# GpSimd adds half of the expert planes between the first layer and the scan, the third norm goes by logarithm and exponential, and zeros are written in the routing

## The reference, cut to what matters

```
x: 16 sequences x 256 steps x 128 features, float32 (4096 tokens)
x = x + 0.5 * ffn(layernorm(x))      # first layer
x = x + mamba(layernorm(x))          # the scan
x = x + 0.5 * ffn(layernorm(x))      # last layer, same weights as the first

ffn(x): each token goes to its 3 best of 64 experts, at most 64 tokens per expert;
        gelu(x w1 + b1) w2 + b2, times the token's gate, added up over the 3 choices
mamba(x): raw, gate = split(x W_in);  h = silu(conv(raw) + b)
          ts, B, C = split(h W_x);    dt = softplus(ts W_dt + b_dt)
          state = exp(dt * A) * state + dt * B * h     # for 256 channels x 16 states
          y = sum over states (C * state) + h * D;     out = (y * silu(gate)) W_out
```

## Time and profile before

| what | value |
|---|---|
| three runs | 808.17, 806.54, 804.46 us; median 806.54 us |
| the profiled execution | 807.02 us, of which the span of the core 805.1 us |
| mean granted TensorE clock | 0.927 of full |
| busy share of the span | PE 82%, DVE 74%, ACT 57%, POOL 62% |
| first layer, to the last scatter | 0 to 184 us |
| bridge | 184 to 235 us |
| scan | 234.76 to 595.7 us |
| last layer and output | 596 to 805 us |

### The profile page before, as it was taken

One profiled execution on the slowest core, in us unless ns is written; L12 is line 12 of the kernel. 1 busy time (PEld: TensorE's weight loads), 2 busy tenths in 40 slices (PEclk: granted clock), 3 DMA queues, 4 the chain that ended last, 5 costly groups with the idle time before them and its releaser, 6 DMA issues. The chain is left out here.

```text
span 805.1 us, 27454 instructions
## 1 busy us (share of the span) xinstructions
PE 658.1 (82%) x11512; PEld 372.2 (46%) x11512; DVE 597.1 (74%) x1004; ACT 456.3 (57%) x949; POOL 495.6 (62%) x315
## 2 busy tenths in 40 slices
PE   6538998995968889899998989878989169999955
PEld 3524554562434445454544545444546045555532
DVE  7893444453689999999999999978999944533435
ACT  2402554461787888878797987866724004445530
POOL 3104565540138999999999999989961125555520
PEclk7858999997988999999999999999999569999987
DMA  8996999627275332545445153442009708997529
GB/s 279 379 345 195 324 317 313 213 80 276 74 171 118 91 99 58 136 107 136 108 120 121 34 147 68 135 107 57 3 3 357 274 11 259 320 335 249 167 85 351
DMA packets 87971, 141.29 MB, mean 175 GB/s; under 512 B 9587, under 2 KB 34813, under 8 KB 86576
## 3 DMA queue, kind: packets, MB, share of 16 engines
q1 hardware_dynamic: 83440, 126.99, 51.5%
q0 software_dynamic: 4416, 12.65, 4.4%
HBM read 112.16 MB, written 27.71 MB: 174 GB/s over the span
## 5 line engine op out<-in xcount | busy, mean ns | idle before, releaser
L1388 POOL TENSOR_TENSOR BIG<-BIG,R 128x1024 f32<-128x1024 f32 x127 | 305.3, 2437 | 17.5 <-DVE BIG L1309 16.5
L1309 DVE TENSOR_TENSOR_SCAN BIG<-BIG,ps 128x1024 f32<-128x1024 f32 x128 | 285.5, 2269 | 16.9 <-PE ps L933 16.4
L933 PE MATMUL ps<-BIG,stack 64*32 64x128 f32 x8192 | 153.9, 279 | 32.6 <-DVE BIG L1309 21.6
L933 PEld LDWEIGHTS ps<-BIG,stack 64*32 64x32 f32 x8192 | 117.9, 107 | 106.4 <-DVE BIG L1309 71.7
L791 POOL DMA_INDIRECT y_dram<-BIG,row_idx x64 | 64.8, 1013 | 87.1 <-DVE BIG L727 45.2
L777 POOL DMA_INDIRECT R<-xn_dram,tok_idx x64 | 65.4, 1022 | 70.7 <-DVE choice L701 51.7
L727 DVE TENSOR_SCALAR BIG<-ps,row_gate 128x128 f32<-128x128 f32 x64 | 22.2, 348 | 98.7 <-remote 56.6
L1178 ACT ACTIVATE BIG<-R,An 128x510 f32<-128x510 f32 x128 | 84.2, 710 | 4.4 <-DVE BIG L1309 4.3
L1178 ACT ACTIVATE BIG<-BIG,An 128x510 f32<-128x510 f32 x128 | 83.7, 709 | 0.2
L412 ACT ACTIVATE BIG<-ps 128x128 f32<-128x128 f32 x64 | 16.9, 265 | 105.9 <-PE ps L541 76.3
L418 ACT ACTIVATE BIG<-BIG 128x512 f32<-128x512 f32 x64 | 40.0, 625 | 61.2 <-DVE BIG L718 43.3
(11 more groups left out here) (184 smaller groups left out, 908.1 us busy)
## 6 DMA issues: line engine op xcount, KB each, us to landing
BIG<-in_L_ffn_w SPq DMA_DIRECT2D x120, 512.0 KB
BIG<-dt_dram SPq DMA_DIRECT2D x32, 256.0 KB, 4.6
R<-c_dram SPq DMA_DIRECT2D x32, 256.0 KB, 7.6
R<-dt_dram SPq DMA_DIRECT2D x32, 256.0 KB, 4.8
y_dram<-zeros SPq DMA_DIRECT2D x3, 2048.0 KB, 21.7
BIG<-y_dram SPq DMA_DIRECT2D x24, 256.0 KB, 7.5
BIG<-y_dram SPq DMA_DIRECT2D x12, 512.0 KB, 8.1
y_dram<-zeros SPq DMA_DIRECT2D x6, 1024.0 KB, 8.2
```

Of the source, the lines that this page charges most:

```text
L933: last = nc.tensor.matmul(ps[CW * slot:CW * slot + CW, 2 * (st % 2) + b, :] .rearrange("p (g k s) -> p k g s", g=2, k=4)[:, k], dT[q % 2][ ...
L1309: nc.vector.tensor_tensor_scan(state[st % 3], dA[:, st % 6].rearrange("p b g t -> p (b g t)"), ps[:, u:u + 2, :].rearrange("p b n -> p (b ...
L1388: nc.gpsimd.tensor_tensor(prod[st % RP], state[st % 3].rearrange("p (b g t) -> p b g t", b=2, g=2), Cf[q % 2][:, 2 * gp:2 * gp + 2].rearra ...
```

## The change

It has three parts, all within the bridge and the places where the zeros are written.

1. **The sums of planes.** VectorE adds groups 0 and 1 by itself (three adds each). TensorE and VectorE share only groups 2 and 3, and TensorE does each in two halves (`part`). GpSimd adds groups 4 to 7 by itself (`moe_sum_pool`): each group as two halves of 256 elements, three planes each, so 24 instructions, in which one waits for the plane before of its own half. They stand at the head of GpSimd's list for the mamba layer, ahead of the first `dtu`. VectorE's statistics of group g wait for the semaphore `x_pool`. ScalarE's `decays(0)` no longer waits for the sums itself but only for the memset. On ScalarE `xt_copy(0)` now stands ahead of the second root, and both `raw_copy(0, ...)` ahead of `normalise(1)`.
2. **The third norm.** The thirteen instructions are replaced: VectorE adds epsilon (`log_root_opened`, in the old place, ahead of the first scan), ScalarE takes the logarithm and the exponential of minus half of it (`log_root_scalar`, behind `decays(3)`), and VectorE does one Newton step and the mean's term in four instructions (`log_root_closed`, behind the first scan).
3. **The zeros** of the last layer's planes are written as in the first layer: three transfers of 2 MB in SP's list of the last layer, behind the first weight loads; the six transfers in the scan are gone.

```
-SUM_GROUPS = ((1, 2, 3, 4, 5, 6, 7), (1, 3, 5))
+SUM_GROUPS = ((2, 3), (1, 3, 5))
+POOL_GROUPS = (4, 5, 6, 7)
...
+        def log_root_opened(S, i0, i1):
+            nc.vector.tensor_scalar(rs[:, 0, i0:i1], mv[:, i0:i1, 1], EPS, None, ALU.add).then_inc(S("rstd"), 1)
+        def log_root_scalar(e, S, i0, i1, n, m):
+            e.wait_ge(*S.at("rstd", n + 1))
+            nc.scalar.activation(rs[:, 2, i0:i1], rs[:, 0, i0:i1], ACT.Ln).then_inc(S("root"), 1)
+            e.wait_ge(*S.at("root", m + 1))
+            nc.scalar.activation(rs[:, 2, i0:i1], rs[:, 2, i0:i1], ACT.Exp, scale=-0.5).then_inc(S("root"), 1)
+        def log_root_closed(e, S, i0, i1, n, m):
...
+            e.wait_ge(*S.at("root", m + 2))
+            nc.vector.tensor_tensor(y, z, z, ALU.mult).then_inc(S("rstd"), 1)
...  (two scalar_tensor_tensor for y and r, one for nmr)
-            if f == 0:
-                for k in range(K):
-                    e.dma_start(y_dram[0][k * T:(k + 1) * T, :]...
+            for k in range(K):
+                e.dma_start(y_dram[f][k * T:(k + 1) * T, :]...
...
+        def moe_sum_pool(e, S, f, m):
+            g = POOL_GROUPS[m]
+            e.wait_ge(G(f"yk{PIECE[g]}"), 16 * K * (f + 1))
+            for k in range(K):
+                for half in range(2):
+                    i = 4 * g + 2 * half
+                    t = X[:, i:i + 2, :].rearrange("p i d -> p (i d)")
+                    if k:
+                        e.wait_ge(*S.at("pool_partial", 4 * m + 2 * k + half - 1))
+                    nc.gpsimd.tensor_tensor(t, t, YK[:, k, i:i + 2, :].rearrange("p i d -> p (i d)"), ALU.add)\
+                        .then_inc(S("x_pool" if k == K - 1 else "pool_partial"), 1)
...
             root_scalar(e, MST, 0, 4, 0)
             normalise(0)
+            xt_copy(0)
             root_scalar(e, MST, 4, 8, 6)
-            xt_copy(0)
-            normalise(1)
             raw_copy(0, 0)
             raw_copy(0, 1)
+            normalise(1)
...
             decays(3)
+            log_root_scalar(e, MST, 8, NI, 12, 2)
             normalise(2)
...
-            moe_sum(e, F[0], 0, 4)
-            stats(8, 20)
+            stats(8, 24)
...
-            stats(20, NI)
-            statistics(8, NI, 12)
+            stats(24, NI)
+            wait(e, "meanvar", NI)
+            log_root_opened(MST, 8, NI)
             wait(e, "pads", 4)
...
                     if run:
                         scan(STEPS * q + n)
+                    if q == 0 and n == 0:
+                        log_root_closed(e, MST, 8, NI, 12, 2)
                     if q == 0 and n < C2:
                         dt(1, n)
```

More of the change, by code:

```diff
@@ L241, in macaron @@
         w2v = w2.rearrange("(a j) (p c) d -> j p a (c d)", a=2, c=HC)
[L244 to L250, removed]
-            v, y, z, r = rs[:, 0, i0:i1], rs[:, 1, i0:i1], rs[:, 2, i0:i1], rstd[:, i0:i1]
[L253 to L261, removed]
@@ new lines, in log_root_closed @@
+        def log_root_closed(e, S, i0, i1, n, m):
+            v, y, z, r = rs[:, 0, i0:i1], rs[:, 1, i0:i1], rs[:, 2, i0:i1], rstd[:, i0:i1]
+            e.wait_ge(*S.at("root", m + 2))
+            nc.vector.tensor_tensor(y, z, z, ALU.mult).then_inc(S("rstd"), 1)
+            e.wait_ge(*S.at("rstd", n + 2))
+            nc.vector.scalar_tensor_tensor(out=y, in0=y, scalar=-0.5, in1=v, op0=ALU.mult, op1=ALU.mult)\
+                .then_inc(S("rstd"), 1)
+            e.wait_ge(*S.at("rstd", n + 3))
+            nc.vector.scalar_tensor_tensor(out=r, in0=y, scalar=1.5, in1=z, op0=ALU.add, op1=ALU.mult)\
+                .then_inc(S("rstd"), 1)
+            e.wait_ge(*S.at("rstd", n + 4))
+            nc.vector.scalar_tensor_tensor(out=nmr[:, i0:i1], in0=mv[:, i0:i1, 0], scalar=-1.0, in1=r,
+                                           op0=ALU.mult, op1=ALU.mult).then_inc(S("rstd"), 1)
@@ L985, in mamba_tensor @@
                                  start=True, stop=True)
-            for g in range(1, 3):
-                plane_sums(e, F[0], 0, g)
+            plane_sums(e, F[0], 0, 2, 0)
             e.wait_ge(M("pads"), 3)
@@ L991, in mamba_tensor @@
             transposes(0)
-            plane_sums(e, F[0], 0, 3, 0)
+            plane_sums(e, F[0], 0, 2, 1)
             raw(0, 0)
             raw(0, 1)
+            plane_sums(e, F[0], 0, 3, 0)
+            transposes(1)
             plane_sums(e, F[0], 0, 3, 1)
-            transposes(1)
-            plane_sums(e, F[0], 0, 4)
             x_proj(0)
@@ L1080, in normalise @@
                 if q < 3:
-                    wait(e, "rstd", (6, 12, 12 + NEWTON)[q])
+                    wait(e, "rstd", (6, 12, 17)[q])
                 for j in range(4):
@@ L1258, in stats @@
                 for i in range(i0, i1):
-                    if i % 4 == 0:
+                    if i % 4 == 0 and i // 4 in POOL_GROUPS:
+                        e.wait_ge(*F[0].at("x_pool", 2 * POOL_GROUPS.index(i // 4) + 2))
+                    elif i % 4 == 0:
                         e.wait_ge(*F[0].at("x", i // 4 + 1))
@@ L1264, in stats @@
                     nc.vector.bn_aggr(mv[:, i, :], st[:, i, :]).then_inc(M("meanvar"), 1)
-            def statistics(i0, i1, n):
-                wait(e, "meanvar", i1)
-                inverse_root(e, MST, i0, i1, n)
             for u in range(2):
@@ L1340, in mamba_vector @@
                 tap(1, m // 3, m % 3)
-            for g in range(5, 8):
-                moe_sum(e, F[0], 0, g)
-            e.wait_ge(*F[0].at("x", 8))
+            e.wait_ge(*F[0].at("sum", 2))
+            e.wait_ge(*F[0].at("x", 4))
+            e.wait_ge(*F[0].at("x_pool", 8))
             nc.vector.memset(dA[:, :, :, :, 0:1].rearrange("p u b g t -> p (u b g) t"), 0.0).then_inc(M("pads"), 1)
@@ L1405, in diagonal @@
                     .then_inc(M("diag_pool"), 1)
+            for m in range(len(POOL_GROUPS)):
+                moe_sum_pool(e, F[0], 0, m)
             for q in range(-2, NQ):
```

25 lines of the change are left out of this document (6 added, 19 removed).

## The result

| | before | after |
|---|---|---|
| median of 4 runs each, same chip | 807.36 us | 820.09 us |
| range | 804.46 to 811.29 | 818.57 to 826.36 |
| profiled execution: time, span | 807.02, 805.1 | 826.36, 824.6 |
| mean granted TensorE clock | 0.927 | 0.901 |

The change makes the kernel slower: the ratio is 1.0163, with an interval of 1.0102 to 1.0224. The forecast was 808.1 (803.2 to 812.2) with 0.16 for slower. Another series of runs on another chip gave 1.0120 [1.0077, 1.0162]. The profiled execution after is the longest of its four, 6.3 us over their median, so its stages show rather more of the loss than the median has.

What follows compares the result with a forecast made beforehand. Bound: full VectorE and GpSimd in the scan, a chain of hand-overs in the bridge. +1.3 and +0.3 make +1.6 us on the profiled 807.02, so 808.6; the median is 0.5 lower: 808.1, range 803.2 to 812.2.

Steps and rivals of the forecast that it cites:

- rival 2: A TensorE stall in bridge or scan goes or comes as its list shortens; 3.4 us either way, chance 0.14 for better.
- rival 3: Bridge: TensorE too idle, clock at 1.2 GHz again between 203 and 233; half of it costs 4.8 us; chance 0.16.
- The sum of the parts: Whole kernel: 1.3 us for the later second scan step plus 0.3 for GpSimd, +1.6 us.
- To the first silu: Bridge, sums up to the first silu: 1.1 us later, at 210.6 (bounds +0.5 and +1.9).
- GpSimd's adds: Bridge: 24 adds on GpSimd at 0.72 us each, 17.3 us in all, done at 218.8; cost counted 0.
- From silu to the decays: Bridge: 0.4 of the 1.1 us delay comes back, decays start at 229.8; first scan step at 233.4, 1.3 earlier.
- The third norm: Start of the scan: second step waits for ScalarE's exponential, at 240.6, 1.3 us later (bounds +0.7 and +2.1).
- GpSimd late by 0.3: Start of the scan: GpSimd's `dtu` and first product start 2.9 us later; 0.3 us added (0 to 0.8).
- The zeros: Zeros moved from the scan to the last layer: cost 0, bounds -1 and +1 us.
- the same: Whole kernel: measured time within 0.5%, 4.0 us, of before, between 802.5 and 810.6; chance 0.74.

Runs made afterwards that it cites:

- the kernel before with 205 added: The kernel before with 205 waiting TensorE instructions added, 145 in the first layer's routing and 60 in the bridge; ratio 1.0102 to the kernel before.
- with the edges back in place: The kernel after with 51 waiting TensorE instructions added in the bridge; 787.17 us, ratio 1.0019 to the kernel before on the same chip.
- With the clock kept: The kernel after with 25 matmuls on ones and one waiting instruction added in the bridge; 810.02 us, ratio 0.9996 to the kernel before.

## Why the prediction was wrong

**The step that failed is rival 2, a stall of TensorE that goes or comes.** It saw what decides: long waits with nothing named "look like instructions that came late", and with 24 matmuls and their weight loads out of the list "every later stall falls elsewhere". But it priced this as one stall, with 3.4 us either way, and gave a chance of its own only to the better side; for slower it counted on rival 3 "with some stalls". Measured, the other place cost 1.4% or about 11.6 us in the first series (1.0163 / 1.0019), about 8 us in the second (1.0120 / 1.0019) and by the kernel before with 205 added (1.0102). The missing step is that the list repeats: a block is nearly 9 pieces long, so a bad place is bad in every block. That much stood in the trace of the kernel before: the count of TensorE's instructions between equal steps of two blocks, 2294, and the places of its three unnamed stalls in the list, which all leave 254 when divided by 256. Whether the new place is better or worse could not be read from that; it takes the place of the transfers in the block as well.

**The sum of the parts held as a whole.** +1.6 us was forecast; with the edges back in place it is +1.5 (-0.9 to +3.9). That the two agree so closely is in part luck, as its terms held less well:

- *To the first silu*, +1.1 forecast: counted from the last scatter it is about +0.3. The four refining instructions behind the second root took 0.41, 0.65, 0.65 and 0.65 us instead of 0.16, 1.7 more in all, close to the 2 I took and short of the 2.8 of a full add for each: two-input instructions of VectorE do get slower beside GpSimd's adds. But group 2 was in at 196.8, not 197.6, and the two raw copies ended at 204.54, not 206.2; VectorE had the second root (204.06) and a sum (204.8) done in time.
- *GpSimd's adds*: 0.72 forecast, 16.43 / 24 = 0.68 measured, done at 217.02; cost 0, as said.
- *From silu to the decays*: first step forecast at 233.4, measured at 235.51, with 5.49 us of waiting for TensorE. This is rival 3: the granted clock was 0.50 from 211 to 214 and from 218 to 231, and the two `x_proj` took 3.17 and 3.73 us. With the clock kept the bridge is 1.4 us shorter and the first step 1.4 earlier than before, so in that profile the forecast of this step (1.3 earlier) holds but for the clock. I had set the rival at 4.8 us, and that sum was wrong in itself: its terms, with 1.9 for each `dt_proj`, add up to 11.4 and not 9.5, so half of it is 5.7.
- *The third norm*: the hole of 3.02 us ended by the exponential, the second step at 242.18 against 240.6. The shape is right; the 1.6 us come from the first step, 2.1 late. That it costs 3.2 us alone was outside my bounds; open, as said.
- *GpSimd late by 0.3*: no run isolates it.
- *The zeros*: 0 forecast, 0.9992 [0.9967, 1.0017].

**The chances.** "The scan's length is fixed by work that the change leaves alone" was the sentence on which the 0.74 for "the same" rested, and it was false: the change leaves the scan's work alone, not the place of its code. The earlier trace rows showed a total of 16.4 us of waits with a longest of 3.4, and I took them as given.

## What to carry to other kernels

Where an engine works through tens of thousands of unrolled instructions, count what a change adds to or takes from its list, and what the length of the repeated block leaves when divided by 256. If the block is near a multiple, compare the change at a fixed place of the edges (fill up with waits that are already met) before judging it, and try a few places: here they are worth from -0.6% to over +1%, more than the change. In the trace look for long "issue" waits at equal distances in the list, and for data transfers that run while the next piece of code is due.

## What the runs showed of the hardware

- TensorE's code comes in 16 KB pieces by DMA. A piece due while 2 MB of row and C transfers (eight of 256 KB) were in flight came 9.2 us after the one before it instead of some 4; at the five such places TensorE stood 2.3 to 4.4 us, and went on 2.7 to 2.9 us after the piece's start.
- Instructions that do nothing but wait for a condition already met shift the edges as well as matmuls do: adding 20 of them made the kernel before, 808.7 us on that chip, some 4.5 us faster (0.9944).
- VectorE instructions of 0.16 us with two inputs in SBUF took 0.65 while GpSimd added 256 elements at 0.68 us each.
- TensorE's granted clock went from 1.00 to 0.50 at about 211 us, after waits of 1.11 and 2.28 us between its instructions, and stayed at 1.00 up to 230 us with 25 matmuls put in between.
